# Layer 4's queries and keys as two fp32r words on half of the array's rows, two heads side by side

## The reference

```python
    def _L1_xattn_ref(query, key, value, Wq, bq, Wk, bk, Wv, bv, Wo, bo):
        ...
        q = split_heads(query @ Wq.T + bq)      # 16 heads of 16
        k = split_heads(key @ Wk.T + bk)
        v = split_heads(value @ Wv.T + bv)
        scores = jnp.einsum('bhqd,bhkd->bhqk', q, k) / np.sqrt(HEAD_DIM)
        weights = jax.nn.softmax(scores, axis=-1)
        out = jnp.einsum('bhqk,bhkd->bhqd', weights, v)
        out = out.transpose(0, 2, 1, 3).reshape(b, -1, D_MODEL)
        return out @ Wo.T + bo
```

## Time and profile before

| | |
|---|---|
| median of 3 runs | 2451.73 us (2449.49 to 2453.33) |
| profiled execution | 2446.4 us, its span 2445.1 us |
| mean granted TensorE clock | 0.906 |
| PE busy | 1991.8 us (81%) |
| DVE busy | 1796.9 us (73%) |
| ACT busy | 1184.3 us (48%) |
| POOL busy | 640.7 us (26%) |
| wide attention | 0 to 330 us |
| mixer with keys and values | about 330 to 950 |
| mixture of experts | to 1280 |
| layer 4: start, loop | 1280 to 1400, 1400 to 2207 |
| causal attention, MLP | to 2445 |

### The profile page before, as it was taken

How to read it: one execution, slowest core, us unless ns; L and a number is a source line. 1 busy time by engine, 2 the same in 40 slices (tenths; PEclk the granted TensorE clock), 3 DMA queues, 4 the chain that set the end, 5 groups by cost and what they waited for, 6 DMA issues and landing times. The chain is left out here.

```text
span 2445.1 us, 35575 instructions
## 1 busy us (share of the span) xinstructions
PE 1991.8 (81%) x12719; PEld 1278.3 (52%) x12745; DVE 1796.9 (73%) x2462; ACT 1184.3 (48%) x2000; POOL 640.7 (26%) x292
## 2 busy tenths in 40 slices
PE   7999977766676664999982799999999999998564
PEld 6778844444454443878871144445445554445323
DVE  6777345999999984566537787888878878844675
ACT  1333337644564423344310166667767776673262
POOL 3433021666667521232205000000000000004522
PEclk8999989988898877999995599999999999998776
DMA  7455332333333312121105944555655655501000
GB/s 260 158 193 201 104 95 91 112 112 101 110 111 100 120 52 94 55 74 57 39 10 93 126 70 70 86 80 78 90 86 78 88 78 82 93 1 48 13 0 18
DMA packets 128360, 215.63 MB, mean 88 GB/s; under 512 B 10544, under 2 KB 93872, under 8 KB 125120
## 3 DMA queue, kind: packets, MB, share of 16 engines
q1 hardware_dynamic: 126464, 212.86, 38.1%
q10 hardware_dynamic: 1728, 0.49, 0.1%
HBM read 168.75 MB, written 44.56 MB: 87 GB/s over the span
## 5 line engine op out<-in xcount | busy, mean ns | idle before, releaser
L1836 DVE TENSOR_REDUCE xn_peaks<-psum 128x1 f32<-128x512 f32 x1024 | 634.1, 683 | 146.3 <-PE psum L1674 146.3
L1816 ACT ACTIVATE xn_weights<-psum 128x512 f32<-128x512 f32 x1024 | 538.5, 602 | 233.7 <-PE psum L1700 232.0
L1674 PE MATMUL psum<-xn_k_stack,xn_q_stack 96*128 96x512 bf16 x1024 | 400.1, 398 | 34.6 <-DMA xn_q_stack<-q_parts 29.6
L1700 PE MATMUL psum<-xn_q_stack,xn_k_stack 99*128 99x256 bf16 x2048 | 387.1, 275 | 17.3 <-issue 8.8
L1700 PEld LDWEIGHTS psum<-xn_q_stack,xn_k_stack 99*128 99x128 bf16 x2048 | 179.0, 98 | 216.2 <-ACT xn_weights L1816 77.1
L1713 PE MATMUL psum<-xn_weights,xn_v 128*32 128x256 f32 x4096 | 278.5, 386 | 4.5 <-issue 4.3
L1658 POOL COPY xn_v<-xn_v_in 128x2048 f32<-128x2048 f32 x16 | 30.3, 1893 | 791.5 <-DMA xn_v_in<-v_all 791.5
L1103 DVE TENSOR_TENSOR_SCAN mx_state<-mx_decay,mx_state 128x1024 f32<-128x1024 f32 x64 | 215.0, 3360 | 0.0
L864 POOL TENSOR_TENSOR mx_state<-mx_du,mx_b_all_channels 128x1024 f32<-128x1024 f32 x64 | 179.3, 2802 | 0.7
L1032 ACT ACTIVATE mx_decay<-mx_delta,mx_a 128x512 f32<-128x512 f32 x128 | 85.4, 715 | 182.1 <-DVE mx_state L1103 182.1
L1713 PEld LDWEIGHTS psum<-xn_weights,xn_v 128*32 128x32 f32 x4096 | 114.7, 109 | 109.5 <-issue 70.1
(11 more groups left out here) (331 smaller groups left out, 3211.7 us busy)
## 6 DMA issues: line engine op xcount, KB each, us to landing
xn_k_stack<-k_parts SPq DMA_DIRECT2D x192, 256.0 KB, 9.8
k_parts<-ctx_k_parts SPq DMA_DIRECT2D x64, 384.0 KB, 2.7
xw_mask<-in_mask_BxSxS_ik SPq DMA_DIRECT2D x8, 2048.0 KB, 7.6
xw_ctx_natural<-in_ctx SPq DMA_DIRECT2D x32, 512.0 KB, 5.9
ctx_chunk<-in_ctxT SPq DMA_DIRECT2D x32, 512.0 KB, 4.2
v_all<-ctx_v SPq DMA_DIRECT2D x32, 512.0 KB, 3.1
moe_w<-in_L_ffn_w SPq DMA_DIRECT2D x16, 1024.0 KB, 5.3
xn_v_in<-v_all SPq DMA_DIRECT2D x16, 1024.0 KB, 16.1
```

The lines of the kernel that those rows point to most:

```text
L1674: pe.matmul(PS[:, x % 3, :], t["Q"][0:XN_PART_ROWS, n % XN_GROUPS * HG + j, b * S + q * P:b * S + (q + 1) * P], t["K"][0:XN_PART_ROWS, n % ...
L1700: last = pe.matmul(PS[:, 3 + y % 3, half * S:(half + 1) * S], t["K"][0:XN_ROWS, n % 2, j, kt * P:(kt + 1) * P], t["Q"][0:XN_ROWS, n % XN_G ...
L1816: act.activation(t["weights"][:, step % 2 * HG + j, :, :], PS[:, 3 + y % 3, :].rearrange("p (t s) -> p t s", t=2), ACT.Exp).then_inc(s.exp ...
L1836: dve.tensor_reduce(t["peaks"][:, n % 2, j, q, c:c + 1], PS[:, x % 3, :], AX.X, ALU.max).then_inc(s.max_dve, 1)
```

## The change

Queries and keys are now split into two fp32r words instead of three bf16 parts. A head has three stacked products and two shift rows: 50 rows (`XN_ROWS`), which fit in half of the array. Heads 2p and 2p + 1 stand on rows 0 to 49 and 64 to 113 (`narrow_rows`), and their matmuls are issued one after the other, into two banks.

- The keys: ACT rounds each block twice instead of three times, PE makes one remainder (in fp32r) instead of two; `k_words` in DRAM holds two fp32 words.
- The queries: the projection's weights are laid out on the host with each head's columns three times, so that PE writes the queries to all rows where they are wanted (32 units of a batch and two heads, L1692 of the new kernel). ACT copies each unit twice, as an fp32r word and whole (L1829, L1833), POOL subtracts in place for the rows of the low word (L1653). The units are made between the M of group 0. DVE's splitting and the way through DRAM are gone. The factor 1/4 moves into the exponential.
- The waits on banks now ask for the last but one: `x - 1` of pairs in place of `x - 2` of single ones.
- S is one block for the four heads, fp32 with the fp32 identity, and stands after W of step 14. DVE makes two words with three operations instead of six.
- On SP's queue wo, bo and bv come after the keys and values of group 0. `dt_w` of the mixer moves into a part of another buffer.

```diff
-    k.K_parts = k.nc.dram_tensor("k_parts", (B, 3, D, S2), BF16, kind="Internal").ap()
+    k.K_words = k.nc.dram_tensor("k_words", (B, 2, D, S2), F32, kind="Internal").ap()
...
-    def remainder(i, m, n):
-        pe.wait_ge(kr[m], 3 * i + n)
-        pe.matmul(PS[:, banks[m], :], t["minus"][:], t["parts"][:, m, n - 1, :], start=False, stop=True,
+    def remainder(i, m):
+        pe.wait_ge(kr[m], 2 * i + 1)
+        pe.matmul(PS[:, banks[m], :], t["minus"][:], t["keys"][:, m, 0, :], start=False, stop=True,
                   skip_group_check=True).then_inc(kp[m], 1)
 
     def values(i, pair):
         if sub == 0:
             keys(i, 0)
         elif sub == 1:
-            remainder(i, 0, 1)
+            remainder(i, 0)
             keys(i, 1)
         elif sub == 2:
-            remainder(i, 0, 2)
-            remainder(i, 1, 1)
+            remainder(i, 1)
             values(i, 0)
...
-XN_PART_ROWS = 6 * XN_DH
-XN_ROWS = XN_PART_ROWS + 3
-XN_Q_PART, XN_K_PART = (0, 1, 2, 0, 1, 0), (0, 0, 0, 1, 1, 2)
+XN_PAIRS = XN_HEADS // 2
+XN_HALF = P // 2
+XN_SHIFT = 32
+XN_LOW = XN_SHIFT + 2
+XN_ROWS = XN_LOW + XN_DH
+XN_KEY_ROWS = ((0, 0), (XN_DH, 1), (XN_LOW, 0))
 XN_HALVES = 2
 XN_SCALE = XN_DH ** -0.5
 XN_N = B * XN_GROUPS
-XN_MAXIMA = [(c, j, q) for c in range(CH) for j in range(XN_HEADS) for q in range(QT)]
-XN_SLOTS = (XN_STEPS - 1) * XN_HEADS
+XN_UNITS = B * XN_GROUPS * XN_PAIRS
+XN_MAXIMA = [(c, p, q) for c in range(CH) for p in range(XN_PAIRS) for q in range(QT)]
+XN_SLOTS = (XN_STEPS - 1) * XN_PAIRS
...
-        for r in range(6):
-            sp.dma_start(t["K"][r * DH:(r + 1) * DH, n % 2, :, cols],
-                         k.K_parts[b, XN_K_PART[r], g * HG * DH:(g + 1) * HG * DH, cols].rearrange(
-                             "(h i) s -> i h s", h=HG)).then_inc(keys[n % 2][half], 16)
+        for at, word in XN_KEY_ROWS:
+            for a in range(2):
+                sp.dma_start(t["K"][narrow_rows(a, at, at + DH), n % 2, :, cols],
+                             k.K_words[b, word, g * HG * DH:(g + 1) * HG * DH, cols].rearrange(
+                                 "(p a i) s -> a i p s", p=XN_PAIRS, a=2)[a]).then_inc(keys[n % 2][half], 16)
...
+    sp.dma_start(t["wq"][:], d["L1_xattn_WqS"].rearrange("(k p) a n -> p k a n", p=P)).then_inc(s.weights, 16)
+    sp.dma_start(t["bq"][:], d["L1_xattn_bqS"]).then_inc(s.weights, 16)
+    load_keys(0, 0)
+    load_keys(0, 1)
     load_values(0)
+    sp.dma_start(t["wo"][:], d["L1_xattn_WoT"].rearrange("(k p) n -> p k n", p=P)).then_inc(s.weights, 16)
+    for n in ("bo", "bv"):
+        sp.dma_start(t[n][:], d["L1_xattn_" + n].rearrange("(a d) -> a d", a=1).partition_broadcast(P)).then_inc(
+            s.weights, 16)
...
+    def key_ones(slot):
+        for a in range(2):
+            pool.memset(t["K"][narrow_rows(a, XN_SHIFT, XN_LOW), slot, :, :], 1.0).then_inc(s.ones, 1)
+            pool.wait_ge(s.ones, 2 * slot + a + 1)
+    def query_low(u):
+        pool.wait_ge(s.qx, u + 1)
+        cols = slice(u // (2 * XN_GROUPS) * S, (u // (2 * XN_GROUPS) + 1) * S)
+        for a in range(2):
+            rows = narrow_rows(a, XN_SHIFT)
+            q = t["Q"][rows, u % (2 * XN_GROUPS), cols]
+            pool.tensor_tensor(q, t["qx"][rows, u % 2, :], q.bitcast(F32), ALU.subtract).then_inc(s.qlo, 1)
+            pool.wait_ge(s.qlo, 2 * u + a + 1)
+    def values(n):
         pool.wait_ge(s.values, 16 * (n + 1))
         if n >= 2:
             pool.wait_ge(s.sum_pe, XN_STEPS * (n - 1))
         pool.tensor_copy(t["V"][:, n % 2, :, :, 0:XN_DH], t["Vin"][:].rearrange("p t (h n) -> p t h n", h=XN_HEADS)
                          ).then_inc(s.v, 1)
+    key_ones(0)
+    query_low(0)
+    query_low(1)
+    pool.memset(t["V"][:, :, :, :, XN_DH + 1:], 0.0).then_inc(s.pads, 1)
+    pool.wait_ge(s.pads, 1)
+    pool.memset(t["V"][:, :, :, :, XN_DH], 1.0).then_inc(s.pads, 1)
+    pool.wait_ge(s.pads, 2)
+    values(0)
+    pool.wait_ge(s.v, 1)
+    for u in range(2, 4):
+        query_low(u)
+    key_ones(1)
+    for u in range(4, XN_UNITS):
+        query_low(u)
+    for n in range(1, XN_N):
+        values(n)
...
     def maxima(n, m):
+        c, p, q = XN_MAXIMA[m]
+        b, x = n // XN_GROUPS, 2 * (len(XN_MAXIMA) * n + m)
+        if x >= 2:
+            pe.wait_ge(s.max_dve, x - 1)
+        if m == 0:
+            pe.wait_ge(s.qlo, 4 * (n + 1))
+            pe.wait_ge(s.ones, 2 * min(n + 1, 2))
+        if m % (len(XN_MAXIMA) // XN_HALVES) == 0:
+            pe.wait_ge(keys[n % 2][c * XN_HALVES // CH], 96 * (n // 2 + 1))
+        for a in range(2):
+            pe.matmul(PS[:, (x + a) % 3, :],
+                      t["Q"][narrow_rows(a), n % XN_GROUPS * XN_PAIRS + p, b * S + q * P:b * S + (q + 1) * P],
+                      K[narrow_rows(a), n % 2, p, c * BANK:(c + 1) * BANK], start=True, stop=True).then_inc(s.max_pe, 1)
+    def shift_rows(n):
+        pe.wait_ge(s.shift, 3 * (n + 1))
+        if n:
+            pe.wait_ge(s.rows, 2 * n)
+        if n >= 2:
             pe.wait_ge(s.nmul, QT * (n - 1))
             if (n - 2) % XN_GROUPS == XN_GROUPS - 1:
                 pe.wait_ge(s.xo, QT * ((n - 2) // XN_GROUPS + 1))
+        for a in range(2):
+            for p in range(XN_PAIRS):
+                for q in range(QT):
+                    col = (p * QT + q) * P
+                    last = pe.matmul(PS[narrow_rows(a, XN_SHIFT, XN_LOW), XN_MISC, col:col + P],
+                                     t["neg_words"][:, n % 2, (p * QT + q) * 2 + a, :].bitcast(F32), k.ident[:],
+                                     start=True, stop=True)
+            last.then_inc(s.row_pe, 1)
+    def exponentials(n, step, p):
+        b, y = n // XN_GROUPS, HG * (XN_STEPS * n + step) + 2 * p
+        if y >= 2:
+            pe.wait_ge(s.exp_act, y - 1)
+        if step == 0 and p == 0:
+            pe.wait_ge(s.rows, 2 * n + 2)
         for half in range(2):
             kt = 2 * step + half
+            for a in range(2):
+                last = pe.matmul(PS[:, 3 + (y + a) % 3, half * S:(half + 1) * S],
+                                 K[narrow_rows(a), n % 2, p, kt * P:(kt + 1) * P],
+                                 t["Q"][narrow_rows(a), n % XN_GROUPS * XN_PAIRS + p, b * S:(b + 1) * S],
+                                 start=True, stop=True)
+                if half:
+                    last.then_inc(s.exp_pe, 1)
...
+    for u in range(2):
+        queries(u)
     for m in range(len(XN_MAXIMA)):
         maxima(0, m)
-    for pair in range(HG // 2):
-        shift_rows(0, pair)
+        if m + 2 < XN_UNITS:
+            queries(m + 2)
+    shift_rows(0)
     for n in range(XN_N):
         more = n + 1 < XN_N
         for step in range(XN_STEPS):
-            for j in range(HG):
-                slot = step * HG + j
-                if slot in (1, 3, 5):
-                    finish(n - 1, slot // 2)
-                exponentials(n, step, j)
+            for p in range(XN_PAIRS):
+                slot = step * XN_PAIRS + p
+                if slot in (1, 2, 3):
+                    finish(n - 1, slot - 1)
+                exponentials(n, step, p)
                 if more and slot < XN_SLOTS:
                     for m in narrow_point(slot):
                         maxima(n + 1, m)
-            if more and step == XN_STEPS - 1:
-                shift_rows(n + 1, 0)
             if step:
                 weighted(n, step - 1)
-            if more and step == XN_STEPS - 1:
-                shift_rows(n + 1, 1)
+        if more:
+            shift_rows(n + 1)
         weighted(n, XN_STEPS - 1)
...
+    def queries(u):
+        b, pair = u // (2 * XN_GROUPS), u % (2 * XN_GROUPS)
+        act.wait_ge(s.qpe, u + 1)
+        act.activation(t["Q"][:, pair, b * S:(b + 1) * S], PS[:, 3 + u % 3, 0:S], ACT.Identity,
+                       bias=t["bq"][:, pair:pair + 1]).then_inc(s.qhi, 1)
+        if u >= 2:
+            act.wait_ge(s.qlo, 2 * (u - 1))
+        act.activation(t["qx"][:, u % 2, :], PS[:, 3 + u % 3, 0:S], ACT.Identity,
+                       bias=t["bq"][:, pair:pair + 1]).then_inc(s.qx, 1)
+
+    def shift_rows(n):
+        b, pair = n // XN_GROUPS, n % XN_GROUPS * XN_PAIRS
+        for a in range(2):
+            rows = narrow_rows(a, XN_SHIFT, XN_LOW)
+            act.wait_ge(s.row_pe, 2 * n + a + 1)
+            act.copy(t["Q"][rows, pair:pair + XN_PAIRS, b * S:(b + 1) * S],
+                     PS[rows, XN_MISC, :].rearrange("p (h s) -> p h s", h=XN_PAIRS)).then_inc(s.rows, 1)
...
+        dve.wait_ge(s.max_dve, 2 * len(XN_MAXIMA) * (n + 1))
+        if n >= 2:
+            dve.wait_ge(s.row_pe, 2 * (n - 1))
+        words = t["neg_words"][:, n % 2, :, :]
+        dve.tensor_reduce(t["neg"][:], t["peaks"][:, n % 2, :, :], AX.X, ALU.max, negate=True).then_inc(s.shift, 1)
+        dve.wait_ge(s.shift, 3 * n + 1)
+        dve.tensor_copy(words[:, :, 0], t["neg"][:]).then_inc(s.shift, 1)
+        dve.wait_ge(s.shift, 3 * n + 2)
```

(1 more changed line is left out.)

224 lines of the change are left out of this document (69 added, 155 removed).

## The result

The changed kernel takes 2556.0 us (median of four runs, 2549.0 to 2557.2) against 2450.6 (four runs on the same chip): ratio 1.043, interval 1.040 to 1.045, so 105 us slower. Its profiled execution took 2556.7 us (span 2555.4), 110.3 more than that of before.

What follows compares the result with a forecast made beforehand. PE was taken to set the main loop's pace, by little. Mixer -4, start -9 and main loop +39 gave +26 us: 2472 against the profiled execution, 2478 as median; 8 in 10 between 2440 and 2560.

Steps and rivals of the forecast that it cites:

- Mixer: Mixer ahead of layer 4: fewer ScalarE roundings and remainders on PE save 4 us (0 to 9).
- Start: Start of layer 4: first maxima near 1321 us, first exponentials at about 1391, a gain of 9 us.
- Side by side: Main loop: matmuls of two heads on the two row halves run at once, a pair costing the columns of one.
- Exposed load and E's chain: Main loop: weight load behind a wait adds 0.11 us; one pair of exponentials to the next takes 1.20, a step 2.90.
- Doubled slots: Main loop: two slots hold two pairs, each paying the maxima's chain, 2 x 1.28 against 4 x 0.45 us: +0.8.
- Seam: Between two head groups: 5.4 us against 4.42, +1.0, with 1.76 for the shift rows ahead of the weighted sums.
- Last group: Last head group, without maxima: a step of 2.66 us against 2.41, 16 steps, +4 us.
- Main loop by waits: Layer 4's loop: two waits eat PE's 0.75 us saving; +35 us for fifteen groups, +4 for the last, +39.
- Clock: TensorE's clock in the main loop: the forecast's sum held no term for a fall.
- Clock falls: Rival, main loop: a fifth of the loop falls to 1.2 GHz, +75 us, 2550 us; chance 0.13.
- halves in series: Rival, main loop: the row halves run one after the other, step about 3.45 us, +150, 2589 us; chance 0.11.

Runs made afterwards that it cites:

- g1_spare_in_waits: Changed kernel with spare bf16 products that nothing reads, only where TensorE waits ahead of second pairs of exponentials; 2475.2 us.
- h1_64_rows: Changed kernel with each head on 64 array rows instead of 50, the added rows ones in the keys and zeros in the queries; 2494.9 us.
- k1_before_50_rows: Kernel before with maxima and exponentials on 50 rows instead of 96 and 99, exponentials' scale 1e-6; 2765.6 us.
- e4_series: Changed kernel with its two heads issued one after the other again, each with a wait two banks back; 2515.8 us.
- g3_weave_loads: Changed kernel with weighted sums cut in two, half behind each pair, and wo, bo, bv loaded ahead of the first keys; 2430.7 us.
- f3_before_weave: Kernel before with each step's weighted sums cut in two, half behind the second head and half behind the fourth; 2475.1 us.

## Why the prediction was wrong

Forecast 2478 us, +26; measured +105 (+110 by the profiled executions). Step by step:

- **Mixer, -4**: layer 4 began 4.3 us earlier, but that the numbers agree so closely is luck. The mixer's first stretch, up to the scan's first state update, became 6.6 us shorter (315.0 to 431.5 before, 319.0 to 428.9 after; 116.0 to 116.5 us in all four kernels with three parts, 109.7 to 112.9 in all thirteen with two words). The long stretch behind it gained nothing, as forecast (470.1 and 470.7 us), and the stretch from the last update to the experts another 2.4. Against this the wide attention, which the change does not touch, ended 4.0 us later in this execution; over the profiled executions of all kernels its end spreads from 314.8 to 319.4.
- **Start, -9**: -5.6, so 3 us less than forecast. First M 1319.9 (forecast 1321), GpSimd's 64 remainders at a median of 722 ns without a gap to 1387.2 (1389). The layer began 4.3 us earlier, but from its first transfer to the first query were 37.4 us, where I had 34.5: 3 of the 4 us went there.
- **Side by side**: right. The two heads' matmuls of a pair start 2 to 4 ns apart in the trace. The Trainium skill (TensorEngine Tiling (Array Packing), Key Properties) says that tiles work independently; for row halves this trace agrees.
- **Exposed load and E's chain**: right, 1.19 us for 1.20. The second half of a step is 1.75 us for 1.70, so the step is 2.94 for 2.90.
- **Doubled slots**: 4.22 us (2.94 + 1.28), as forecast. (Before, the fifth M's 0.45 us was not a gapless stream, as I read it: half of it is PE waiting for VectorE. The term is a measured one and stands.) **Seam**: 4.91 for 5.4; the 16 transposes take 1.2 us, where I had 1.76 from W's rate. **Last group**: 2.62 for 2.66.
- **Main loop by waits, +39**: +27 at the full clock. The median steps of a group add up to 51.6 us against 49.0, which gives 39 for 15 groups and 3 for the last (forecast 35 and 4). But before had nine single steps 0.6 to 2.2 us too long, 14 us in all, in which PE waited for nothing that the profile shows; g1_spare_in_waits had two, 2 us. Why is open. Three kernels agree on the loop at full clock: 834, 833 (g1_spare_in_waits) and 832 us (h1_64_rows, 852 - 56 x 0.36), against 806 of before.
- **Clock, 0**: this is the step that failed. The half clock cost (268 - 10) x 0.36 = 93 us. The sum -4.3 - 5.6 + 27 + 93 is 110, the whole difference; the 27 is what the 93 leave of the loop's 120, and the three loops at the full clock check it.

The rival "Clock falls" had this and near its size (+75), at 0.13. I judged it by how long PE streams: the last group of before kept 1.00 with 1.7 of 2.41 us, and 1.9 of 2.90 seemed little worse. The runs show that the comparison lacked the rows: the last group streamed on 99 rows, the changed kernel on 50, in pairs. k1_before_50_rows changed the rows (and W's data) and nothing of the rhythm, and the clock went to 0.61; h1_64_rows gave the changed kernel 64 rows, and it came back to 0.97. The earlier trace rows held a hint, 40 us at 0.50 with PE busy 37.5 of them: a busy PE in the records and a low clock do go together. Those were maxima on 96 rows, so rows are not all that counts, and what exactly the clock answers to stays open.

The Trainium skill (TensorE: Matmul & The Clock Gate, What's actually happening) says that the clock follows how busy TensorE has lately been. With spare work the trace agrees (g1_spare_in_waits); if busy is taken from the records, it does not: k1_before_50_rows fell out of a stretch with PE busy 96 of 99 us, and h1_64_rows kept 0.97 with 573 of 700. The measurement decides.

Of the other rivals, "halves in series" was priced at steps of 3.45 and 2589 us; e4_series made it real and took 2.95 us a step, since the waits two banks back return with it.

## What to carry to other kernels

When a change makes TensorE's work thinner (fewer rows of the array, shorter streams), price the clock as a term of its own, and test it by filling the rows or the waits with work that nothing reads. A saving on the engine that is the bound is only had if its order lets it be used: two heads at a time on three banks wait for each other unless other work stands between them. Spare or reordered work is free only where the trace shows a wait right behind it.

## What was not expected of the hardware

- Rows of the array that hold only zeros on one side and ones on the other keep the clock up: 50 to 64 rows a half, 0.86 to 0.97 in the loop, 61 us.
- The same instructions ran at either level for a long time: k1_before_50_rows had whole head groups at 5.39 us a step and others at 2.84. Some such kernels spread by 38 to 92 us between runs (g3_weave_loads, k1_before_50_rows, e4_series), where before spreads by 10; the changed kernel, with 268 us at half, spreads by 8.
- A change of the tile shape of TensorE costs about 0.12 us each way between 128-row products of 32 columns and the score matmuls (f3_before_weave, 3.10 - 2.86 for one cut, which adds two changes).
